# Causal attention of a fused decoder kernel: a step's scores written in one run over whole PSUM banks, both units attended in one run, the output bias added to the residual rows by GpSimd

## Chip, cores and metric

The kernel runs on one core of a Trainium2 chip. The metric is the device time of one execution in microseconds; lower is better. The core has five engines with a queue of instructions each: TensorE (PE in the profile, its weight loads PEld), VectorE (DVE), ScalarE (ACT), GpSimd (POOL) and SyncE (SP), which here only starts transfers.

## The reference, cut to what matters

Two decoder layers over 64 sequences of 64 tokens with 128 features. The change touches one sublayer, the causal self-attention of the second layer (16 heads of 8 features):

```python
def _L1_attn_ref(x, Wq, bq, Wk, bk, Wv, bv, Wo, bo):
    q = split_heads(x @ Wq + bq)
    k = split_heads(x @ Wk + bk)
    v = split_heads(x @ Wv + bv)
    att = jnp.einsum('bhqd,bhkd->bhqk', q, k) * scale
    att = jnp.where(tril, att, -inf)
    att = jax.nn.softmax(att, axis=-1)
    y = jnp.einsum('bhqk,bhkd->bhqd', att, v)
    return y @ Wo + bo
...
x = x + _L1_attn_ref(_layernorm(x, axis=-1), ...)
```

Everything is float32.

## The kernel before, in words

The program is written by hand, engine by engine, one stage after another; engines meet only at semaphores, and each engine works through its own list in order. The stage in question is `causal_attention`. The tokens lie as 32 tiles of 128 rows in the tensor `X`. A step takes two tiles, that is four sequences; there are 16 steps. The four sequences of a step are two units of two sequences.

What a step n does, and on which engine:

- POOL: `combine` adds the routed experts' results of the sublayer before to the two tiles of `X` (three operations, L2197, L2202, L2208); `root` takes the reciprocal root of the norm's variance (L154).
- DVE: `stats` (L141 to L148) and `normed` (L161) are the norm; the normed rows go to `xn`.
- PE: `turn_rows` transposes them (L1945), ACT `rows` copies them to `hT`; PE `project_qk` makes queries and keys (L1953), ACT `copies_q` and `copies_k` spread them over head slots (L2107, L2112), two instructions each; PE `project_v` makes the values (L1961), ACT `spread_v` copies them.
- PE `score`: for one unit, 16 small matmuls of 32 rows by 32 columns write the causal mask's bias over 256 columns of banks 0 to 3 (L1977), and 8 matmuls with 32 rows add the products of queries and keys (L1982). Each float32 matmul appears as two records in the trace. Both units use the same half of the four banks, so a unit's scores can be written only when DVE has read those of the unit before (`less_top`).
- DVE `softmax`: the largest of each row (L2284) and the difference (L2287); ACT `exp` (L2133).
- PE `turn`: four transposes of a quarter of a step's probabilities (L1992), written to the one bank `TURN_BANK`; ACT `copy_turned` copies them out (L2128). A step has four such turns, named by unit and half: 0,0; 0,1; 1,0; 1,1.
- PE `attend`: for one unit, probabilities by values and probabilities by ones (L2009), into `ATTN_BANK`; DVE `normalise` takes the reciprocal (L2292) and multiplies (L2294).
- PE `project`: a matmul of ones by a row that holds the output bias (L2021) starts the sum, two matmuls (L2023) add the output projection; DVE `add` adds the result to `X` (L2299).

`run_steps` writes the order. Its body for step n also works on the norm of later steps and on the end of earlier ones. The order of PE's body before, in a middle step: scores of unit 0; turn 1,0 of step n-1; project n-2; turn 1,1 of n-1; attend unit 0 of n-1; project_qk of n+1; scores of unit 1; project_v of n; turn 0,0 of n; attend unit 1 of n-1; turn 0,1 of n; turn_rows of n+2. Steps 3 to 10 run in a hardware loop with two steps in a turn, the others are written out. The last body and the one before it also make keys, values and queries of the next stage (`next_...`).

## Time and profile before

| | us |
|---|---|
| median of 3 runs | 1831.68 |
| lowest and highest | 1824.25, 1832.2 |
| the profiled execution's own time | 1832.89 |
| its span, from first to last instruction | 1831.1 |
| PE busy in the span | 1726.8 (94%) |
| DVE busy | 1202.5 (66%) |
| ACT busy | 895.7 (49%) |
| POOL busy | 617.2 (34%) |
| mean granted clock of TensorE, share of full speed | 0.982 |

The times in rows of the trace are counted from the start of the span. The stage of the change lies from about 1205 to 1396 us. Busy time leaves out waiting. Matmul records overlap, since one enters the array while the one before drains; the distance from the start of one group to the start of the next says what a group costs on PE, and the record's own length is longer by the drain.

### The profile page before, as it was taken

Reading aid. Unit: us, or ns where it says so; the run is one execution under the profiler, and the core shown is the slowest. Engines: PE = TensorE matmul, PEld = TensorE weight load, DVE = VectorE, ACT = ScalarE, POOL = GpSimd, SP = SyncE. Lnnn points to the kernel's source line nnn. Section 1 sums busy time; section 2 is a strip of 40 time slices with the busy share of each in tenths; the row PEclk is TensorE's granted clock in tenths of the full one; section 3 lists DMA queues with packets and bytes.
Section 4 is the critical chain, followed back from the end, with each engine's and each line's share of the span. In section 5 each row is a group of like instructions: output and inputs, shape, how many; then the busy total and the mean of one; then the engine's idle time right before and its main releaser. Section 6 shows DMA issues by size and latency. Waiting matters only on the chain. (4 is left out here: it accounts for less than half of the span.)

```text
span 1831.1 us, 49181 instructions
## 1 busy us (share of the span) xinstructions
PE 1726.8 (94%) x19304; PEld 1283.1 (70%) x19304; DVE 1202.5 (66%) x2925; ACT 895.7 (49%) x1930; POOL 617.2 (34%) x744
## 2 busy tenths in 40 slices
PE   6999999998999999999799999989998999999778
PEld 5566666666888888888556668857776777777643
DVE  6677777656777778776452223238887777777757
ACT  1444444446666766666332213347774555445324
POOL 2111111112334344343215523343222444444427
PEclk9999999999999999999999999989999999999979
DMA  9300000002444444444410002210010333333301
GB/s 331 92 1 0 0 0 0 1 1 90 142 144 138 143 143 139 148 139 138 132 57 31 32 20 98 99 54 26 29 37 32 97 104 97 97 100 102 103 29 41
DMA packets 176164, 146.81 MB, mean 80 GB/s; under 512 B 12168, under 2 KB 154299, under 8 KB 175506
## 3 DMA queue, kind: packets, MB, share of 16 engines
q1 hardware_dynamic: 172690, 139.12, 23.7%
q0 software_dynamic: 3328, 5.58, 0.9%
q8 instruction: 111, 1.82, 0.4%
q14 instruction: 35, 0.29, 0.1%
HBM read 79.00 MB, written 67.43 MB: 80 GB/s over the span
## 5 line engine op out<-in xcount | busy, mean ns | idle before, releaser
L1061 ACT ACTIVATE xa_probs<-ps,xa_top 128x128 f32<-128x128 f32 x512 | 145.9, 368 | 149.5 <-DVE xa_top L1164 148.5
L154 POOL TENSOR_TENSOR rstd<-var_eps,minus_half 128x2 f32<-128x2 f32 (+1 forms) x116 | 91.9, 792 | 358.0 <-DVE var_eps L148 357.8
L1105 POOL TENSOR_TENSOR xa_probs<-xa_probs,xa_total 128x512 f32<-128x512 f32 x128 | 133.0, 1039 | 200.5 <-DVE xa_total L1159 200.5
L977 PE MATMUL ps<-xa_probsT,xa_kv 128*128 128x512 f32 x256 | 136.7, 616 | 15.7 <-DMA xa_probsT<-turned_blocks 14.5
L1164 DVE TENSOR_REDUCE xa_top<-ps 128x4 f32<-128x512 f32 x128 | 88.3, 690 | 91.3 <-PE ps L968 90.3
L956 PEld LDWEIGHTS ps<-xa_kvT,pack_latent 128*128 128x128 f32 x512 | 97.2, 192 | 65.9 <-issue 56.9
L987 PEld LDWEIGHTS ps<-pack_latent,xa_attnT 128*128 128x128 f32 x1024 | 134.0, 192 | 11.4 <-issue 5.7
L968 PE MATMUL ps<-xa_kvT,xa_qT 128*128 128x128 f32 x1024 | 135.5, 276 | 1.4 <-ACT xa_probs L1061 1.4
L987 PE MATMUL ps<-pack_latent,xa_attnT 128*128 128x128 f32 x1024 | 134.4, 275 | 0.0
L395 PEld LDWEIGHTS ps<-pack_moe,la_hid 128*128 128x128 f32 x1024 | 121.0, 192 | 17.4 <-issue 15.3
L956 PE MATMUL ps<-xa_kvT,pack_latent 128*128 128x256 f32 x512 | 131.5, 382 | 1.4 <-PEq L343 1.4
L382 PE MATMUL ps<-la_h2T,pack_moe 128*128 128x512 f32 x256 | 129.8, 616 | 3.1 <-ACT la_hid L591 3.1
L968 PEld LDWEIGHTS ps<-xa_kvT,xa_qT 128*128 128x128 f32 x1024 | 124.8, 192 | 2.4 <-issue 2.1
L591 ACT ACTIVATE la_hid<-ps,pack_moe 128x512 f32<-128x512 f32 x128 | 86.9, 686 | 80.2 <-PE ps L382 78.4
L395 PE MATMUL ps<-pack_moe,la_hid 128*128 128x128 f32 x1024 | 125.2, 278 | 0.0
L2669 POOL TENSOR_TENSOR ba_probs<-ba_probs,ba_top 128x512 f32<-128x512 f32 x64 | 67.2, 1051 | 142.6 <-DVE ba_top L2736 142.6
L2482 PE MATMUL ps<-ba_inT,pack_latent 128*64 128x128 f32 x1920 | 114.7, 277 | 0.3 <-ACT ba_qT_odd L2595 0.3
L1508 DVE TENSOR_TENSOR rt_mid<-ps,rt_silu 128x512 f32<-128x512 f32 x64 | 44.2, 690 | 106.6 <-ACT rt_silu L1362 106.6
L2482 PEld LDWEIGHTS ps<-ba_inT,pack_latent 128*64 128x64 f32 x1920 | 103.4, 137 | 9.0 <-DVE ba_qT_odd L2746 1.5
L1362 ACT ACTIVATE rt_silu<-ps 128x512 f32<-128x512 f32 x64 | 38.1, 597 | 124.1 <-PE ps L1325 124.1
L1157 DVE TENSOR_REDUCE xa_total<-xa_probs 128x4 f32<-128x512 f32 x128 | 84.1, 657 | 18.3 <-ACT xa_probs L1061 17.3
L1152 DVE STREAM_TRANSPOSE xa_blocks<-xa_probs 128x512 f32<-128x512 f32 x128 | 90.3, 705 | 1.2 <-POOL xa_probs L1105 1.2
(349 smaller groups left out, 3759.7 us busy)
## 6 DMA issues: line engine op xcount, KB each, us to landing
turned_blocks<-xa_blocks SPq DMA_DIRECT2D x128, 256.0 KB, 3.2
xa_probsT<-turned_blocks SPq DMA_DIRECT2D x128, 256.0 KB, 3.0
turned_blocks<-ba_blocks SPq DMA_DIRECT2D x64, 256.0 KB, 2.5
ba_probsT<-turned_blocks SPq DMA_DIRECT2D x128, 128.0 KB, 2.7
expert_weights<-experts_dram SPq DMA_DIRECT2D x8, 768.0 KB, 5.4
result_pairs<-zeros SPq DMA_DIRECT2D x1, 4096.0 KB, 29.4
ca_got<-result_pairs SPq DMA_DIRECT2D x16, 256.0 KB, 2.7
slot_rows<-zeros SPq DMA_DIRECT2D x1, 2880.0 KB, 18.2
```

Source lines behind the costliest of these rows:

```text
L154: pool.tensor_tensor(m.rstd[:, 0:tiles], m.var_eps[:, 0:tiles], m.minus_half[:, 0:tiles], ALU.pow).then_inc(sem.rstd, 1)
L382: pe.matmul(HIDDEN[n % 2], w["w1"][:, n // F0, n % F0, :], h2T[:], start=True, stop=True)\
L395: mm = pe.matmul(out, hid[:, n % 2, f, P * t:P * t + P], w["w2"][:, n, f, :], start=(f == 0), stop=(f == F0 - 1))
L956: mm = pe.matmul(bank(PROJ_BANK + n % 2)[:, NS * a:NS * a + NS], qk_fold[:, 2 * n + a, :], kvT[:, k, :, SEQ:], start=True, stop=True)
L968: mm = pe.matmul(bank(u % 2)[:, KEYS * n:KEYS * n + KEYS], qT[:, k, seq, head:head + 2, :].rearrange("p a q -> p (a q)"), kvT[:, k, seq, : ...
L977: pe.matmul(bank(ATTN_BANK + u % 2), kv[:, k, seq, :], probsT[:, u % SETS].rearrange("p g n q -> p n g q"), start=True, stop=True)\
L987: mm = pe.matmul(bank(OUT_BANK)[:, P * t:P * t + P], attnT[:, t, h, :], vo_fold[:, h, :], start=(h == 0), stop=(h == H - 1))
L1061: exp = act.activation(probs[:, s % 4, n], bank(s % 2)[:, KEYS * n:KEYS * n + KEYS], ACT.Exp, bias=top[:, s % 4, n:n + 1], scale=-1.0)
L1105: pool.tensor_tensor(probs[:, u % 4], probs[:, u % 4], over(total[:, u % 4], 2, KEYS), ALU.mult).then_inc(probs_ready, 1)
L1152: dve.transpose(blocks[:, u % SETS], probs[:, u % 4].rearrange("p n (j k) -> p j n k", k=QUARTER))\
L1164: dve.tensor_reduce(top[:, s % 4], scores, AX.X, ALU.min).then_inc(top_ready, 1)
L2482: mm = pe.matmul(proj_bank(n)[SEQ * seq:SEQ * seq + SEQ, P * h:P * h + P], (w["bq"], w["bk"])[n // 4][:, at:at + DHX], tokens[:, seq], sta ...
```

## The change

- `score(step, k)` handles both units: 16 bias matmuls over all 512 columns of the four banks, then 16 matmuls of queries and keys. `scores_done` rises once a step. The run waits for the subtraction of both units of the step before; that wait stands ahead of the last transpose of `turn 0,0`.
- DVE's `softmax` of unit u reads columns 256u to 256u+255 of the banks.
- PE's order in a body becomes: scores; turn_rows of n+1; turn 0,1 of n-1; project n-2; turn 1,0 of n-1; project_qk of n+1; turn 1,1 of n-1; attend unit 0 and unit 1 of n-1; project_v of n; turn 0,0 of n.
- ACT's order becomes: rows of n+1; copy_turned 0,1 and 1,0 of n-1; exp of unit 0 of n; copy_turned 1,1 of n-1; copies_q and copies_k of n+1; spread_v of n; copy_turned 0,0 of n; exp of unit 1 of n.
- DVE's `stats` is done a step further ahead (step n+3) and at the end of a body, behind `normalise`.
- The bias matmul leaves `project`. Ahead of the steps PE makes the bias as 128 equal rows, ACT copies them to `bias_rows`, and POOL's new `add_bias` adds them to the two tiles of `X` after their norm has read them; DVE's `add` waits for that.

```diff
-                def score(step, k, u):
+                def score(step, k):
...
-                            pe.matmul(bank(g)[QUARTER * c:QUARTER * c + QUARTER, 0:NS], w["ident"][rows, rows],
-                                      over(w["causal_bias"][rows, c % 2, :], 1, 2 * QP), start=True, stop=False)
-                    for b in range(2):
+                            pe.matmul(bank(g)[QUARTER * c:QUARTER * c + QUARTER, :], w["ident"][rows, rows],
+                                      over(w["causal_bias"][rows, c % 2, :], 1, SB * QP), start=True, stop=False)
+                    for b in range(SB):
...
-                def turn(step, u, b):
+                def turn(step, u, b, scored_next=None):
...
+                        if j == J - 1 and scored_next is not None:
+                            score_inputs(scored_next)
...
-                    pe.matmul(bank(ROW_BANK)[:, 0:NS], w["ones"][:], out_bias[:], start=True, stop=False)
                     for t in range(2):
                         mm = pe.matmul(bank(ROW_BANK)[:, P * t:P * t + P], attnT[:, P * t:P * t + P], w["co"][:],
-                                       start=False, stop=(t == 1))
+                                       start=True, stop=True)
...
@@ tensor engine, body(step, k, ahead)
                     if here:
-                        score(step, k, 0)
+                        score(step, k)
...
+                    if ahead >= 1:
+                        turn_rows(later(step, 1), 1 - k)
                     if before:
-                        turn(later(step, -1), 1, 0)
+                        turn(later(step, -1), 0, 1)
                     if has(step, 2):
                         project(later(step, -2), ahead)
                     if before:
+                        turn(later(step, -1), 1, 0)
+                    if ahead >= 1:
+                        project_qk(later(step, 1), 1 - k)
+                    if before:
                         turn(later(step, -1), 1, 1)
...
                     if before:
+                        attend(later(step, -1), 1 - k, 0)
                         attend(later(step, -1), 1 - k, 1)
                     if here:
-                        turn(step, 0, 1)
+                        project_v(step, k)
+                    if here:
+                        turn(step, 0, 0, later(step, 1) if ahead >= 1 else None)
...
@@ scalar engine, body
+                    if ahead >= 1:
+                        rows(later(step, 1), 1 - k)
                     if before:
+                        copy_turned(later(step, -1), 0, 1)
                         copy_turned(later(step, -1), 1, 0)
-                        copy_turned(later(step, -1), 1, 1)
                     if here:
                         exp(step, 0)
+                    if before:
+                        copy_turned(later(step, -1), 1, 1)
...
@@ gpsimd
+                def add_bias(step):
+                    rows = m.X[:, 2 * step:2 * step + 2, :]
+                    pool.wait_ge(ln.normed, 2 * step + 2)
+                    pool.tensor_tensor(rows, rows, over(bias_rows[:], 1, 2), ALU.add).then_inc(bias_added, 1)
...
                 for step in range(4, STEPS):
                     pool.wait_ge(ln.normed, 2 * step)
                     combine(step)
+                    add_bias(step - 2)
                     root(step)
...
@@ vector
                 def add(step):
+                    dve.wait_ge(bias_added, count(step, 1, 1))
                     dve.wait_ge(out_done, count(step, 1, 1))
...
                     if before:
                         normalise(later(step, -1), 1 - k)
+                    if ahead >= 3:
+                        stats(later(step, 3))
```

## Rows read from the trace of the kernel before

**Rows 1.** The page: busy time of each engine over the whole span

```profile
PE 1726.8 (94%) x19304; PEld 1283.1 (70%) x19304; DVE 1202.5 (66%) x2925; ACT 895.7 (49%) x1930; POOL 617.2 (34%) x744
```

**Rows 2.** Windows: length, busy us (and records) of PE, PEld, DVE, ACT, POOL; clock

```profile
1301.01:1310.94 9.93, 9.93 (x272) 7.42 (x268) 8.68 (x16) 7.35 (x16) 3.24 (x5) 1.00 0.08 26
1377.50:1396.30 18.80, 16.41 (x425) 13.04 (x423) 15.37 (x32) 7.70 (x15) 1.01 (x1) 1.00 0.01 3
```

**Rows 3.** Timeline, DVE: the softmax that opens steps 1, 2 and 14, last add

```profile
1234.12 1.23 DVE L2284 TENSOR_REDUCE ca_top<-ps 128x16 f32<-128x1024 f32 x1 [0.32 <-PE ps L1982]
...
1244.97 1.22 DVE L2284 TENSOR_REDUCE ca_top<-ps 128x16 f32<-128x1024 f32 x1
...
1365.16 1.21 DVE L2284 TENSOR_REDUCE ca_top<-ps 128x16 f32<-128x1024 f32 x1
...
1395.89 0.42 DVE L2299 TENSOR_TENSOR X<-ps,X 128x256 f32<-128x256 f32 x1 [0.66 <-PE ps L2023]
```

**Rows 4.** Timeline, PE, one step in the middle: start, length, engine, line

```profile
1303.65 0.71 PE L1977 MATMUL ps<-pack_later_constants,pack_constants 32*32 32x256 f32 x32
1304.30 0.74 PE L1982 MATMUL ps<-ca_kpairs,ca_qpar 32*128 32x128 f32 x16
1304.99 0.65 PE L1992 MATMUL ps<-pack_constants,ca_probs 128*128 128x128 f32 x4
1305.48 0.60 PE L2021 MATMUL ps<-ca_out_bias,pack_constants 128*128 128x256 f32 x2
1305.92 0.61 PE L2023 MATMUL ps<-pack_causal,ca_attnT 128*128 128x128 f32 x4
1306.36 0.63 PE L1992 MATMUL ps<-pack_constants,ca_probs 128*128 128x128 f32 x4
1306.92 0.43 PE L2009 MATMUL ps<-ca_probsT,ca_vheads 128*32 128x64 f32 x16
...
1307.95 1.13 PE L1953 MATMUL ps<-ca_hT,pack_causal 128*128 128x256 f32 x4
1309.01 0.71 PE L1977 MATMUL ps<-pack_later_constants,pack_constants 32*32 32x256 f32 x32
...
1310.33 0.69 PE L1961 MATMUL ps<-pack_causal,ca_hT 128*64 128x64 f32 x16
```

**Rows 5.** Timeline, ACT, the same step

```profile
1307.03 0.60 ACT L2128 ACTIVATE ca_probsT<-ps 128x512 f32<-128x512 f32 x1 [0.75 <-PE ps L1992]
1307.68 1.06 ACT L2133 ACTIVATE ca_probs<-ca_probs 128x1024 f32<-128x1024 f32 x1
1309.12 1.02 ACT L2107 ACTIVATE ca_qpar<-ps,ca_qbias,pack_constants 128x256 f32<-128x256 f32 x2 [0.38 <-PE ps L1953]
1310.03 1.02 ACT L2112 ACTIVATE ca_kpairs<-ps,ca_kbias,pack_constants 128x256 f32<-128x256 f32 x2
```

**Rows 6.** Timeline, DVE, from the last operation before the second softmax on

```profile
1309.36 0.60 DVE L161 TENSOR_SCALAR ca_xn<-X,mean_var,rstd 128x128 f32 x2 [0.44 <-POOL rstd L154]
1310.45 1.22 DVE L2284 TENSOR_REDUCE ca_top<-ps 128x16 f32<-128x1024 f32 x1 [0.49 <-PE ps L1982]
...
1312.92 1.75 DVE L2292 RECIPROCAL ca_rden<-ps 128x256 f32<-128x256 f32 x1
...
1315.30 1.23 DVE L2284 TENSOR_REDUCE ca_top<-ps 128x16 f32<-128x1024 f32 x1 [0.18 <-PE ps L1982]
```

**Rows 7.** Timeline, PE: the first scores of step 0, and what follows

```profile
1220.97 1.17 PE L1977 MATMUL ps<-pack_later_constants,pack_constants 32*32 32x256 f32 x32 [0.60 <-ACT ca_kpairs L2112]
...
1223.24 3.21 PE L1914 MATMUL ps<-pack_latent,ba_inT 128*128 128x512 f32 x4
```

**Rows 8.** All instructions of a line or tile: ns min/median/max, first and last start

```profile
L2208 POOL TENSOR_TENSOR X<-X,ca_got x16: 722/731/741, 1213.6 to 1352.2; 128x256 f32<-128x256 f32 x16
```

**Rows 9.** Timeline of the next stage, DVE, then POOL in the same microseconds

```profile
1410.64 1.32 DVE L2724 TENSOR_SCALAR ba_xn<-X,mean_var,rstd 128x128 f32<-128x128 f32 x2
...
1410.80 1.08 POOL L2669 TENSOR_TENSOR ba_probs<-ba_probs,ba_top 128x512 f32<-128x512 f32 x1 [0.28 <-DVE ba_top L2736]
```

More of the change, by code:

```diff
@@ L1946, in turn_rows, with project_qk @@
                     mm.then_inc(hT_turned, 1)
-                def project_qk(step, k, scored):
+                def project_qk(step, k):
                     pe.wait_ge(hT_ready, count(step, 1, 1))
                     for n in range(2):
-                        if n == 1 and scored is not None:
-                            score_inputs(scored, 1)
                         mm = pe.matmul(bank(QK_BANK)[:, NS * n:NS * n + NS], w["cqk"][:, n, :], hT[:, k, :],
@@ L2028, in body @@
                     here, before = ahead >= 0, has(step, 1)
-                    if not before or ahead == 0:
-                        score_inputs(step, 0)
+                    if not before:
+                        score_inputs(step)
                     if here:
-                        score(step, k, 0)
+                        score(step, k)
                     if not before:
@@ L2035, in body @@
                         next_values(7)
-                        turn_rows(later(step, 1), 1)
+                    if ahead >= 1:
+                        turn_rows(later(step, 1), 1 - k)
                     if before:
-                        turn(later(step, -1), 1, 0)
-                    if before and not has(step, 2):
-                        turn_rows(later(step, 1), 1 - k)
+                        turn(later(step, -1), 0, 1)
                     if not here:
@@ L2045, in body @@
                     if before:
+                        turn(later(step, -1), 1, 0)
+                    if not here:
+                        next_queries(2)
+                    if ahead >= 1:
+                        project_qk(later(step, 1), 1 - k)
+                    if before:
                         turn(later(step, -1), 1, 1)
[L2047 to L2049 removed]
                     if ahead == 0:
                         next_rows()
[L2052 to L2061 removed]
                     if before:
+                        attend(later(step, -1), 1 - k, 0)
                         attend(later(step, -1), 1 - k, 1)
                     if here:
[L2065 removed]
+                        project_v(step, k)
+                    if not before:
+                        pe.wait_ge(kv_copied, 8)
+                    if here:
+                        turn(step, 0, 0, later(step, 1) if ahead >= 1 else None)
                     if ahead == 0:
                         next_queries(0)
[L2068 to L2071 removed]
                     if not here:
@@ L2079, in _ @@
                     .then_inc(offsets_done, 1)
-                pe.matmul(bank(1)[0:1, 0:D], w["c_bias"][:, 2:3], w["co"][:], start=True, stop=False)
-                pe.matmul(bank(1)[0:1, 0:D], w["ones"][0:1, 0:1], w["bo"][0:1, :], start=False, stop=True).then_inc(out_bias_done, 1)
+                pe.matmul(bank(1)[:, 0:D], over(w["c_bias"][:, 2], 1, P), w["co"][:], start=True, stop=False)
+                pe.matmul(bank(1)[:, 0:D], w["ones"][0:1, :], w["bo"][0:1, :], start=False, stop=True).then_inc(out_bias_done, 1)
                 next_context()
@@ L2147, in body @@
                         copy_next_kv(7)
+                    if ahead >= 1:
+                        rows(later(step, 1), 1 - k)
                     if before:
+                        copy_turned(later(step, -1), 0, 1)
                         copy_turned(later(step, -1), 1, 0)
-                        copy_turned(later(step, -1), 1, 1)
-                    if not before:
-                        rows(later(step, 1), 1)
                     if here:
                         exp(step, 0)
+                    if before:
+                        copy_turned(later(step, -1), 1, 1)
                     if ahead >= 1:
                         copies_q(later(step, 1), 1 - k)
-                    if ahead >= 1:
                         copies_k(later(step, 1), 1 - k)
@@ L2172, in body @@
                         act.activation(biased.inT[:].rearrange("p a n -> p (a n)"), next_q_bank(0), ACT.Copy).then_inc(biased.in_ready, 1)
-                    if ahead >= 2:
-                        rows(later(step, 2), k)
                 act.wait_ge(offsets_done, 1)
@@ L2180, in _ @@
                 act.wait_ge(out_bias_done, 1)
-                act.wait_ge(zeroed, 2)
-                act.activation(tiles_of(out_bias[0:1, :]), over(bank(1)[0:1, 0:D], 1, 2), ACT.Copy).then_inc(out_bias_ready, 1)
+                act.activation(bias_rows[:], bank(1)[:, 0:D], ACT.Copy).then_inc(out_bias_ready, 1)
+                act.wait_ge(zeroed, 1)
                 for n in range(4):
@@ L2224, in _ @@
                 root(2)
+                pool.wait_ge(out_bias_ready, 1)
+                add_bias(0)
+                add_bias(1)
                 root(3)
@@ L2228, in _ @@
                     combine(step)
+                    add_bias(step - 2)
                     root(step)
+                add_bias(STEPS - 2)
+                add_bias(STEPS - 1)
                 for first in range(2):
@@ L2307, in body @@
                         softmax(step, 0)
-                    if ahead >= 2 and has(step, 2):
-                        stats(later(step, 2))
                     if not before:
@@ L2321, in body @@
                         normed(later(step, 2))
-                        stats(later(step, 3))
                     if ahead in (0, 1):
```

45 lines of the change are left out of this document (14 added, 31 removed).

## The prediction

> **What bounds the kernel now.** I read the page first: PE is busy 94% of the span, every other engine far less [rows 1]. That is an average over seven stages, so next came the windows of this stage. In a middle step of 9.93 us PE is busy all 9.93 us, DVE 8.68, ACT 7.35, POOL 3.24 [rows 2]. The reader is to see two things: PE sets the pace, and DVE stands only 1.25 us behind it, so no saving on PE above about 1.1 us a step can come through. The timeline of DVE gives the pace over the whole stage: from the first softmax of step 2 at 1244.97 to that of step 14 at 1365.16 are 12 steps in 120.19 us, 10.02 each, 0.09 above the dense step (the hardware loop's turn and small waits); from there to the end of the last `add` at 1396.31 are 31.15 us [rows 3]. The last stretch is looser: PE is busy 16.41 of its last 18.80 us [rows 2]. Then the timeline of PE, for what each piece costs from start to start: scores of a unit 1303.65 to 1304.99, 1.34 us, of which 0.65 the bias matmuls and 0.69 the products, and again 1.32 for the other unit (1309.01 to 1310.33); a turn 0.49; the output bias 0.44; the projection 0.44; a turn that is followed by attention 0.56; attention of a unit 1.03; `project_qk` 1.06; `project_v` to the end of the step 0.61 [rows 2, 4]. Last, ACT and DVE, for who hands over to whom: a copy of turned probabilities starts 0.67 us after its transposes start (1306.36, 1307.03) and takes 0.60 [rows 4, 5]; DVE waited 0.49 and 0.18 us for scores in this step [rows 6].
>
> **The change part by part.** The sum is made against the profiled execution (1832.89, its span 1831.1, 1.8 outside it); that lies 1.2 above the median of 1831.68, and I subtract the gain from the median.
>
> *Scores in one run.* The bias matmuls are 16 in place of twice 16 and twice as wide; the products keep number and width. Per step the columns that stream are the same; what goes is one entry and one exit of the run. The 0.65 us of 256-column bias matmuls hold two rounds of streaming, and a whole-array matmul shows the price of a round: `project_qk` streams two matmuls of 256 columns in 1.06 us [rows 4], at most 0.53 each, of which some 0.10 is again entry and exit, so about 0.43. 256 more columns then cost 0.43 more: 0.65 + 0.43 = 1.08. The products: 0.69 holds two rounds of 128 columns (0.43 by the same price) and 0.25 around them, four rounds give 0.86 + 0.25 = 1.11. Together 2.2 against 2.66, **0.46 less**. Bounds: nothing less (2.66, if no entry is saved), or 2 x 0.43 + 2 x 0.43 = 1.7 with nothing around the streaming.
>
> *Output bias.* PE loses L2021: **0.44 less** [rows 4]. POOL gains one operation of 128x256, the same shape as L2208, 0.73 us [rows 8], on an engine busy 3.24 of 9.93 us [rows 2]: it lies beside everything. It is issued behind `combine`, whose result is wanted by a `stats` that is at least 3 us later in my walk below, and DVE's `add` wants it two steps later. If that cover were gone, the 0.73 would delay `stats` and, behind it in DVE's queue, the next softmax. DVE shares something with POOL: in the next stage two norm applications took 1.32 us while a POOL operation ran over them [rows 9], against 0.60 for the same pair here [rows 6]. In the new order POOL starts its chain when `normed` ends and is done some 4 us later, 5 us before the next `normed`, so I price this at nothing and keep 0.72 per step as a rival. The Trainium skill (GPSIMD Engine Reference, Specifications) says that GpSimd shares its SBUF interfaces with VectorE and contends with its two-port modes and with operations of two SBUF inputs; the traces agree with the 1.32 us, and by this rule any meeting of `add_bias` and `normed` would cost that much. The largest and the difference of a softmax were not touched: 1.22 us with POOL running beside it, as elsewhere [rows 3, 6].
>
> *Both units attended in one run, other order on PE.* One entry into the narrow attention matmuls goes (a turn followed by attention takes 0.56, one that is not 0.49, and leaving costs as much: 0.1 together). One entry into the scores goes, counted above. New PE step by start-to-start prices: scores 2.2, two row transposes 0.25 (half a turn), turn 0.49, project 0.44, turn 0.49, `project_qk` 0.9 (no entry into the scores behind it), turn 0.56, attention 1.93, `project_v` 0.61, turn 0.59: **8.46 us**.
>
> *Waits that the order adds.* There is one transpose bank, and turn 0,1 and turn 1,0 now stand in the same body with only `project` between them. Turn 1,0 can start 0.67 + 0.60 + 0.05 = 1.32 us after turn 0,1 has started; turn and projection fill 0.93. So PE stands **0.4 us** there, and all behind it in its queue. Before, such pairs had the attention or the bias matmul between them. New PE step: 8.46 + 0.4 = 8.86, I take 8.9.
>
> The walk of one step, from the end of the scores (0): DVE's difference of unit 0 is done at 2.6. ACT: copy 0,1 at 0.95 to 1.55, copy 1,0 at 2.25 to 2.85, exp of unit 0 at 2.85, next start 0.95 later (exp takes 1.06, the starts overlap a little [rows 5]), copy 1,1 at 3.8 to 4.4, queries at 4.3, keys at 5.2 to 6.2. PE: turn 1,0 at 1.6, `project_qk` at 2.1, turn 1,1 at 2.95, attention of unit 0 at 3.5, of unit 1 at 4.45 (copy 1,1 is just there), `project_v` at 5.45, turn 0,0 at 6.05, whose last transpose waits for keys until 6.25, scores of n+1 at 6.65 to 8.85. DVE: softmax 0 2.5, `add` 0.35 (0.42 long [rows 3], starts overlap), `normed` 0.5 (0.60 long), softmax 1 2.5 (a softmax is 2.47 from start to start [rows 6]), so both units are read at 5.9; then `normalise` until 8.0 (1312.92 to 1315.30 less the 0.18 wait, 2.2 [rows 6]; its attention is done at 5.6) and `stats` until 8.9. The new scores are ready at 8.9. PE, DVE and the chain over ACT all come out at 8.8 to 8.9. With the 0.09 of before: **9.0 us a step, 1.0 less**. DVE's own work, 8.7 to 8.8, is the floor.
>
> *Head.* Step 0 runs at the low clock: its scores of one unit took 2.27 us [rows 7] against 1.34. The doubled run ends 1.7 later at that clock (0.43 x 2 twice), and what follows it partly at the low clock too; against that unit 1 needs no second run. I put the first softmax of step 1 at 1235.2 instead of 1234.12, that of step 2 at 1244.1 instead of 1244.97. Then 12 steps of 9.0: step 14 at 1352.1 against 1365.16, **13.1 us** earlier. `stats` of step n+3 at a body's end is ready long before its `normed`, so the waits of `normed` for POOL's root (0.44 in a step [rows 6]) vanish; that is inside the DVE walk.
>
> *Tail.* Steps 14, 15 and the last body lose twice 0.9 us of PE work, 1.8 at least. The row for the last 18.80 us has 2.4 us of idle PE, and step 14 has 1 more; at most 5.2 goes. The same walk, with the next stage's pieces at their places, gives 27.1 in place of 31.15: **4.0 us**.
>
> Sum: 13.1 + 4.0 = 17.1, so 1831.7 - 17.1 = 1814.6; I say **1815**. Moving the stage's end moves all later stages, whose work does not change.
>
> **Rivals.**
> - *The scores keep their 2.66 us* (the wider matmuls do not overlap so well, or entries cost nothing). Everything behind the scores is 0.46 later a step: 9.45, gain 0.57 x 12 + 3.5 = 10.3, **1821**. For: the rounds' price is from whole-array matmuls. Against: the same columns stream.
> - *Shared access of DVE and POOL*: `normed` meets `add_bias` or `combine`, 0.72 us more on DVE in each of 13 steps, 9.4 us: **1824**. Against: the 5 us between them.
> - *The keys come too late* (slower). The next scores now wait for keys, which on ACT stand behind exp 0 and copy 1,1, which stand behind DVE's softmax; and as the banks are full, DVE has only `normalise` and `stats` to do meanwhile. In my walk keys are there at 6.2, needed at 6.25. Each 0.1 us later costs 0.1 a step. From 1.0 us later (7.2) the gain per step is gone; at 2.0 later the stage is 12 us longer than now less the tail's 4: **1840**. For it: five hand-overs in a row, none with slack; against it: ACT is busy 7.35 of 8.9 us and the hand-overs' times are read from rows.
> - *The waits dissolve*: a turn's copy comes sooner and the step falls to DVE's floor, 8.8, and the tail gives 5: **1811**.
>
> **How the numbers follow.** Forecast 1812 to 1818: 0.58. Falls to the floor: 0.10. Scores keep their time, or chains a little longer: 0.20, of which a quarter lies within 0.5%. Shared access 0.05, within 0.5%. Late keys 0.07, slower but for 0.01. 0.5% is 9.2 us, about what a measurement of this kernel can tell from no change (its three runs spread over 8 us). Faster than 1822.5: 0.58 + 0.10 + 0.15 = 0.83; same 0.11; slower 0.06. The range reaches from the floor less a part of the runs' spread, 1807, to 1823; outside stand shared access, late keys and some noise. The forecast's own range is 1811 to 1818.
>
> **What would show it.** In the changed profile: first softmaxes 9.0 us apart; L1977 with 512 columns, from its start to that of L1982 1.1 us, and 1.1 to the row transposes; an idle of 0.4 before turn 1,0, released by ACT's L2128; no L2021; POOL with one more 0.73 us operation a step; DVE busy over 95% of a step, its wait for scores under 0.2. Wrong if DVE waits for scores by more than 0.5 each step, if PE's last transpose before the scores waits for L2112, or if L161 grows above 0.35 each.

## The result, and the profile after

The changed kernel takes 1819.3 us (median of 12 runs, 1815.3 to 1825.5) against 1829.7 (12 runs, 1824.3 to 1836.6) before. The ratio is 0.9943 with a 95% interval of 0.9926 to 0.9959, that is 10.4 us less; the forecast was 17.1 less. The interval reaches from 0.41% to 0.74%, on both sides of the 0.5% that the prediction calls faster. The profiled execution took 1815.9 us.

The page of the kernel after, busy time by engine, answers to [rows 1]: PE has 22.9 us less, PEld 15.2 less, POOL 12.2 more; DVE and ACT are as they were.

```profile
PE 1703.9 (94%) x18760; PEld 1267.9 (70%) x18760; DVE 1202.5 (66%) x2924; ACT 894.9 (49%) x1930; POOL 629.4 (35%) x760
```

The windows view of the kernel after, one middle step, with the columns of [rows 2]: the step is 9.05 long, PE again busy nearly all of it, POOL 3.91 where it had 3.24.

```profile
1304.30:1313.35 9.05, 9.01 (x238) 6.75 (x235) 8.55 (x16) 7.36 (x15) 3.91 (x5) 1.00 0.09 29
```

The timeline of PE after, one step, to be held against [rows 4]. L1975 is the bias of the scores, L1980 their products, L1993 a turn, L2023 the projection, L2010 the attention.

```profile
1302.11 1.15 PE L1975 MATMUL ps<-pack_later_constants,pack_constants 32*32 32x512 f32 x32
1303.19 1.17 PE L1980 MATMUL ps<-ca_kpairs,ca_qpar 32*128 32x128 f32 x32
1304.30 0.44 PE L1946 MATMUL ps<-pack_constants,ca_xn 128*128 128x128 f32 x2
1304.57 0.60 PE L1993 MATMUL ps<-pack_constants,ca_probs 128*128 128x128 f32 x4
1305.21 0.71 PE L2023 MATMUL ps<-pack_causal,ca_attnT 128*128 128x128 f32 x4
1305.86 0.66 PE L1993 MATMUL ps<-pack_constants,ca_probs 128*128 128x128 f32 x4
...
1307.79 0.43 PE L2010 MATMUL ps<-ca_probsT,ca_vheads 128*32 128x64 f32 x16
...
1309.93 0.69 PE L1960 MATMUL ps<-pack_causal,ca_hT 128*64 128x64 f32 x16
1310.55 0.68 PE L1993 MATMUL ps<-pack_constants,ca_probs 128*128 128x128 f32 x4
1311.16 1.14 PE L1975 MATMUL ps<-pack_later_constants,pack_constants 32*32 32x512 f32 x32
```

From start to start the scores are 1.08 + 1.11 = 2.19 us. From turn 0,1 (1304.57) to turn 1,0 (1305.86) are 1.29 us; the turn and the projection were priced at 0.93, so 0.36 of it is the stand at the one transpose bank. The rows of PE show no idle time there, since each record's length covers the drain; PEld stands 0.27 us before the projection, for ScalarE's copy of the turned rows (L2095), behind which the copy of turn 0,1 lies in ScalarE's queue.

The timeline of DVE after shows the first softmax of two steps, 8.68 apart here and 9.24 in the step before, and `normed` (L161) at 0.60 for the pair. The timeline of POOL after shows the bias addition (L2209), and that POOL is idle while L161 runs.

```profile
1304.79 1.22 DVE L2287 TENSOR_REDUCE ca_top<-ps 128x16 f32<-128x1024 f32 x1 [0.32 <-PE ps L1980]
...
1307.52 0.60 DVE L161 TENSOR_SCALAR ca_xn<-X,mean_var,rstd 128x128 f32 x2
...
1313.47 1.22 DVE L2287 TENSOR_REDUCE ca_top<-ps 128x16 f32<-128x1024 f32 x1
```

```profile
1308.19 1.05 POOL L2188 TENSOR_TENSOR ca_got<-ca_got,pair_weights 128x512 f32<-128x512 f32 x1 [2.94 <-DVE ca_xn L161]
...
1310.82 0.74 POOL L2209 TENSOR_TENSOR X<-X,ca_bias_rows 128x256 f32<-128x256 f32 x1
```

Up to here everything is as in the walk. The distances between first softmaxes over the whole stage show what is not. From step 2 to step 14, in us: 10.26, 10.55, 10.02, 8.80, 9.24, 8.69, 9.24, 8.68, 8.93, 9.79, 9.49, 8.92; then 13.31 from step 14 to step 15. The hardware loop's steps have a mean of 8.93; around them are steps of 10. PE's timeline says why. Two places, one early and one late:

```profile
1242.85 0.40 PE L2010 MATMUL ps<-ca_probsT,ca_vheads 128*32 128x64 f32 x15
1244.37 0.22 PE L2010 MATMUL ps<-ca_probsT,ca_vheads 128*32 128x64 f32 x1 [1.11 <-issue]
...
1355.23 0.33 PE L2010 MATMUL ps<-ca_probsT,pack_later_constants 128*32 128x64 f32 x9
1358.24 0.32 PE L2010 MATMUL ps<-ca_probsT,pack_later_constants 128*32 128x64 f32 x4 [2.68 <-issue]
```

In the middle of a run of equal matmuls, which wait for nobody, TensorE stands. "issue" is time in which no releaser shows. From matmul start to matmul start the stage has five such places: 1.33 us at 1243.03, 1.73 at 1253.39, 1.12 at 1264.56, 2.90 at 1355.35 and 1.38 at 1369.01, together 8.5. Counted in all the instructions that the trace has of TensorE (matmuls, weight loads, and the waits and register operations between them), the first three lie 513 and 512 apart, the last two 513; in matmuls and weight loads alone it is 500, 500 and 508. I call them stands.

For all comparisons the stage is measured alike: from the first matmul of step 0's scores to the end of the last `add`. It is 175.34 us before (1220.97 to 1396.31) and 166.01 after (1216.93 to 1382.94). That is 9.3 less; the other 7.7 of the difference between the two spans (1831.1, 1814.1) lies outside the stage, in work that the change doesn't touch. The stage began at 1216.2 and 1216.3 in two other kernels that keep the order of before (e2, e7), so the 4.0 us earlier start is no gain of the change. Nor, most likely, are some 2 us of the 9.3: the granted clock of TensorE was 0.50 (1.2 GHz) from 1220 to 1225 us in the profile of before and 1.00 (2.4 GHz) in that of the kernel after, and step 2's softmax came 24.0 us after the stage's start in before, 21.8 in e2 and e7. From step 2's softmax to the stage's end there are 151.3 us before and 145.0 after, 6.4 less; a second profile of the kernel after (e5) has 140.0, 11.3 less. The medians' 10.4 lies between the two. One timed run of a later kernel (e2), 5667 us where its eleven others took 1824 to 1834, is left out of its ratio.

### The profile page after: what moved, and what is told of

The parts are those of the page before. It is cut to its first block and busy times, and to the rows that moved or that the text cites. A ratio compares the mean times of both kernels' runs of the same rounds, so it can differ in the third digit from the quotient of the medians.

```text
span 1814.1 us, 48107 instructions
## 1 busy us (share of the span) xinstructions
PE 1703.9 (94%) x18760; PEld 1267.9 (70%) x18760; DVE 1202.5 (66%) x2924; ACT 894.9 (49%) x1930; POOL 629.4 (35%) x760
## 5 line engine op out<-in xcount | busy, mean ns | idle before, releaser
L987 PEld LDWEIGHTS ps<-pack_latent,xa_attnT 128*128 128x128 f32 x1024 | 133.8, 192 | 12.2 <-issue 6.4
```

Source lines behind the costliest of these rows:

```text
L987: mm = pe.matmul(bank(OUT_BANK)[:, P * t:P * t + P], attnT[:, t, h, :], vo_fold[:, h, :], start=(h == 0), stop=(h == H - 1))
```

## The experiments

"Step" is the mean distance of first softmaxes from step 2 to step 14, "loop" the mean of the six loop steps from step 5 to step 11, "stands" the sum inside the stage of the gaps of over 1.1 us from matmul start to matmul start that are put down to issue. All of these are from one profiled execution; the ratio is from timed runs, against the kernel before timed again on the same chip (its medians were 1828.4 to 1833.7 us), so that the ratios can be compared and the times of different groups not.

| kernel | ratio to before (95%) | step | loop | stage | stands |
|---|---|---|---|---|---|
| before | 1 | 10.02 | 10.03 | 175.3 | 0 |
| after | 0.9943 (0.9926 to 0.9959) | 9.38 | 8.93 | 166.0 | 8.5 |
| after, repeated | 0.9917 (0.9885 to 0.9950) | 9.37 | 8.93 | 162.4 | 4.2 |
| bias on TensorE in the new order | 0.9938 (0.9920 to 0.9955) | 9.90 | 9.12 | 169.4 | 8.7 |
| bias alone changed | 0.9997 (0.9979 to 1.0015) | 10.01 | 10.03 | 172.7 | 0 |
| wide ones | 0.9899 (0.9875 to 0.9922) | 8.97 | 8.93 | 157.3 | 0 |
| wide ones, repeated | 0.9918 (0.9890 to 0.9946) | 8.97 | 8.93 | 157.3 | 0 |

**Bias back on TensorE, in the new order (e1).** The kernel after, but with the output bias as a matmul in `project` again and without `add_bias`.

```diff
@@ project
+                    pe.matmul(bank(ROW_BANK)[:, 0:NS], w["ones"][:], out_bias[:], start=True, stop=False)
                     for t in range(2):
                         mm = pe.matmul(bank(ROW_BANK)[:, P * t:P * t + P], attnT[:, P * t:P * t + P], w["co"][:],
-                                       start=True, stop=True)
+                                       start=False, stop=(t == 1))
```

> The changed kernel with the output bias back in TensorE's project (L2021 of before), the order of the change kept. Two theories on where the gain fell short of the forecast (10.4 us measured, 17.1 worked out). Theory F: TensorE runs out of instructions. In the changed profile it stands still five times in the middle of a run of small matmuls, 1.1 to 2.9 us, at places exactly 512 records apart, and the new order puts all small matmuls of a step behind each other. Theory H: the hand-overs to ScalarE and back take longer than in the walk. For this kernel: the bias matmul (0.44 us) now falls into the stand ahead of turn 1,0, where TensorE waits for ScalarE's copy anyway, so both theories expect little: F expects 0 to 3 us more than the changed kernel (ratio to before 0.994 to 0.997), H, with a longer stand, exactly 0. If the bias matmul were on the path in full, it would be 0.44 x 16 = 7 us more: ratio 0.998.

Its loop steps are 9.12 against 8.93: the bias matmul costs 0.19 of a step there, not the 0.44 of [rows 4]. PE's timeline of this kernel shows where the rest is; it stands between turn 0,1 and turn 1,0, where TensorE has to wait anyway.

```profile
1308.11 0.60 PE L1992 MATMUL ps<-pack_constants,ca_probs 128*128 128x128 f32 x4
1308.75 0.70 PE L2021 MATMUL ps<-ca_out_bias,pack_constants 128*128 128x256 f32 x2
1309.28 0.61 PE L2023 MATMUL ps<-pack_causal,ca_attnT 128*128 128x128 f32 x4
1309.73 0.60 PE L1992 MATMUL ps<-pack_constants,ca_probs 128*128 128x128 f32 x4
```

From turn to turn are 1.62 us, 0.33 more than in the kernel after, though L2021 took 0.53 from its start to that of L2023. The stands came here too, five of them, one of 3.28. The ratio (0.9938) can't be told from that of the change.

**The output bias alone, in the order of before (e2).** `project` loses its L2021, POOL gets `add_bias`, the rest is before.

> The kernel before with nothing changed but the output bias: no L2021 on TensorE, add_bias on GpSimd. TensorE is busy all of a step there, so each step should lose 0.44 us: 16 x 0.44 = 7 us, ratio 0.996. If it takes nothing (ratio 1.000), the step of before is held by something else than TensorE's work. Theory F adds that two instructions fewer a step change nothing about fetching here; theory H has nothing to say.

Ratio 0.9997, and every step from 2 to 14 within 0.03 us of that before. PE's timeline of this kernel, turn 1,0, projection, turn 1,1:

```profile
1297.98 0.65 PE L1993 MATMUL ps<-pack_constants,ca_probs 128*128 128x128 f32 x4
1298.47 0.61 PE L2023 MATMUL ps<-pack_causal,ca_attnT 128*128 128x128 f32 x4
1299.33 0.66 PE L1993 MATMUL ps<-pack_constants,ca_probs 128*128 128x128 f32 x4 [0.24 <-ACT ca_probsT L2128]
```

From turn to turn are 1.35 us; before they were 1.37 (1304.99 to 1306.36 in [rows 4]). The bias matmul is gone and an idle of 0.24 <-ACT stands in its place. Two turns through the one transpose bank can't follow each other faster than the transposes, ScalarE's copy and the hand-over: 0.67 + 0.60 + 0.05. In [rows 4] that wait was covered by overlapping records, and it looked like work.

**The same with that wait filled (e11).** `attend` of unit 0 goes ahead of turn 1,1, so that it lies between the two turns; POOL keeps the bias.

```diff
@@ tensor engine, body
+                        attend(later(step, -1), 1 - k, 0)
                         turn(later(step, -1), 1, 1)
-                        attend(later(step, -1), 1 - k, 0)
```

> e2 (the order of before, output bias on GpSimd) with the attention of unit 0 put ahead of the second turn, so that it lies between the two users of the one transpose bank. If the bias matmul was worth nothing in e2 because TensorE stood there for the copy of the first turn's transposes (1.37 us from turn to turn, filled only by 0.44 of projection): that wait goes, a step of 9.5 to 9.6 instead of 10.01, some 6 us less than e2, a ratio of 0.996 to 0.997. If the steps of before are held by something else (VectorE's norms, or the keys): 10.0 again, and the ratio of e2, 1.000.

1826.24 us (12 runs), ratio 0.9967 (0.9947 to 0.9988), step 9.52, stage 165.1. As expected: 0.49 off each step by exchanging two calls. The intervals of the two ratios (this one, and 0.9979 to 1.0015 of e2) just overlap; it is the steps that tell them apart. PE's timeline of this kernel shows projection and attention between the two turns, 2.06 us apart, and no wait:

```profile
1300.65 0.65 PE L1993 MATMUL ps<-pack_constants,ca_probs 128*128 128x128 f32 x4
1301.13 0.61 PE L2023 MATMUL ps<-pack_causal,ca_attnT 128*128 128x128 f32 x4
1301.67 0.43 PE L2010 MATMUL ps<-ca_probsT,ca_vheads 128*32 128x64 f32 x16
...
1302.71 0.66 PE L1993 MATMUL ps<-pack_constants,ca_probs 128*128 128x128 f32 x4
```

**The ones matmuls over both sequences of a unit (e3, again as e10).** After, with the matmuls of probabilities by ones over 128 columns at a time, half as many. The columns that stream are the same, a step has 412 records of TensorE in place of 476, and the attention of both units 192 in place of 256.

```diff
@@ attend
-                        for part in range(2):
...
+                    at = NS + 2 * SEQ * u
+                    for par in range(2):
+                        for j in range(J):
+                            mm = pe.matmul(bank(ATTN_BANK)[FJ * j:FJ * j + FJ, at:at + 2 * SEQ], w["head_ones"][:, par, :],
+                                           probsT[:, u, :, j, SEQ * par:SEQ * par + SEQ],
+                                           start=(par == 0), stop=(par == 1))
```

> The changed kernel with the attention's matmuls by ones done over both sequences of a unit: 128 columns in place of twice 64, half as many of them, the same columns streamed. TensorE's work in time is the same; its records fall by 64 a step of 476, and the dense run of small matmuls is thinner in instructions. Theory F expects the stands inside the run to shrink or vanish: 4 to 7 us less than the changed kernel, ratio to before 0.990 to 0.992. Theory H expects no difference beyond 1 us: ratio 0.994.

> e3 again, unchanged, beside the other two: a ratio of about 0.990, no stand of over 0.6 us inside the steps of its profile, a mean step of 8.9 to 9.0 and a stage of 157 to 158 us. If e3's one profile was a lucky one and the stands come and go: a mean step of 9.2 or more.

1812.22 us and 1816.62 us (6 runs each). The loop steps are those of after to 0.01 us; outside the loop the steps of 10 are gone, both times. One step there is still long, 9.70 and 9.76 us from step 4 to step 5: a stand of 0.75 and of 0.81 us in the values' projection, above the 0.6 that was expected at most for e10. DVE's timeline of the repeat, first softmax of steps 2 and 14 and the last `add`, to be held against [rows 3]:

```profile
1241.17 1.23 DVE L2290 TENSOR_REDUCE ca_top<-ps 128x16 f32<-128x1024 f32 x1 [0.28 <-PE ps L1980]
...
1348.83 1.22 DVE L2290 TENSOR_REDUCE ca_top<-ps 128x16 f32<-128x1024 f32 x1 [0.93 <-PE ps L1980]
...
1375.71 0.42 DVE L2306 TENSOR_TENSOR X<-ps,X 128x256 f32<-128x256 f32 x1 [0.29 <-PE ps L2026]
```

Twelve steps in 107.66 us, 8.97 each (forecast 9.0), and 27.3 from there to the end (forecast 27.1). The waits of TensorE, of the kernel after (1236 to 1383 us) and then of this one (1230 to 1377), as waiting line, releaser, us in total, times, longest:

```profile
PE ps L2010 <- issue: 6.5, 4, 2.7
PE ps L1993 <- ACT ca_probsT L2121: 1.1, 2, 0.7
PE ps L1960 <- issue: 0.9, 1, 0.9
```

```profile
PE ps L1993 <- ACT ca_probsT L2124: 1.7, 3, 0.8
...
PE ps L2026 <- issue: 0.8, 1, 0.8
PE ps L1960 <- issue: 0.6, 1, 0.6
```

The 7.4 us that L2010 and L1960 waited on "issue" have become 0.6, and the stage is 8.7 shorter. Theory H, by which this edit changes nothing, is out.

**The same edit in the order of before (e7).**

> The kernel before with the same edit of the ones matmuls (128 columns, half as many). Its order never stood still for instructions, so theory F expects 0 (ratio 0.999 to 1.001), although TensorE issues 64 records less a step: it is the run of small matmuls that the edit mends, not their number. If fewer records were worth something by themselves, this kernel would gain the 4 us that the edit brought in the new order (ratio 0.997).

1825.88 us (12 runs), ratio 0.9986 (0.9961 to 1.0011). The steps from 2 to 13 are 9.91 to 10.15, those of before. So the edit by itself is worth nothing that can be measured; what it gave in the new order were the stands. This profile has one of the large kind, 4.99 us, in another place than the attention:

```profile
1355.50 0.66 PE L1992 MATMUL ps<-pack_constants,ca_probs 128*128 128x128 f32 x4
1360.87 0.69 PE L1945 MATMUL ps<-pack_constants,ca_xn 128*128 128x128 f32 x2 [4.71 <-issue]
```

**Ones over all four sequences (e6).**

> As the kernel with the wide ones matmuls, and wider: the matmuls by ones are done once a step over all four sequences, 256 columns, 8 of them in place of the changed kernel's 32. TensorE's records fall by another 32 a step (380 against 412 and 476), the columns stay. Theory F: the stands were gone already with 64 records less; so nothing more, 0 to 1 us, and the steps stay 8.9 to 9.0 us, since DVE is the bound (ratio 0.990). If stands of a kind not seen in the profile remained (the run-to-run spread), up to 3 us more. Theory H: again no difference to the changed kernel (0.994).

1810.32 us (6 runs), ratio 0.9887 (0.9855 to 0.9919). One stand, 2.38 us at 1349.07. Its loop steps are 9.16, 0.2 longer than with the edit of e3; why was not followed up.

**Shifting the records (e4, e12).** After, with tiny matmuls put before step 0: 32 of them, which are 128 records, and 128 of them, 512 records. Their result is overwritten.

```diff
@@ before step 0
+                for _ in range(32):
+                    pe.matmul(bank(0)[0:32, 0:8], w["ident"][0:32, 0:32], w["ident"][0:32, 0:8], start=True, stop=True)
```

> The changed kernel with 32 tiny matmuls (128 records) issued by TensorE ahead of step 0, where it waits for keys anyway. They do no work for the result. Everything that follows in TensorE's instruction stream moves by half a block of 256 records. Theory F expects the stands to leave their places (end of the attention of steps 1, 2, 14, 15) and to appear elsewhere, 128 records earlier in the body, and most likely to become shorter, since the ends of two blocks then do not both fall into the dense run: total 0 to 6 us less than the changed kernel. Theory H expects the same places and the same total within 1 us.

> After's order again with tiny matmuls before step 0, as in e4, but 128 of them (512 records in place of 128), which themselves cost some 6 us before the stage more than e4's 2.1. By F (places in TensorE's stream that lie a whole number of blocks apart, whatever stands there): a shift by 512 puts the places back on the instructions on which they lay in after: stands of 1.1 to 1.7 us in the attention matmuls of steps 2 and 3 and in the value projection of step 4, none at those of e4 in the late written-out steps 12 and 13, mean step 9.35 to 9.4, and the clean steps of the loop at 8.68 to 9.24 as before; a large one late in the stage may come or not, as in after and its repeat. If the shift of e4 did something else (another start of the stage, another clock): the stands of e4 again, or none, and a mean step of 9.9 or of 9.0.

With 128 records (1816.79 us, 6 runs, ratio 0.9933, 0.9906 to 0.9960) nothing stands at 1243 to 1265, where steps of 10.3, 10.6 and 10.0 became 9.7, 8.8 and 9.5. Instead TensorE stands in steps that had run freely, 2.03, 1.55 and 4.77 us. They were expected to be shorter; their sum, 8.4, is that of the kernel after. PE's timeline of two of them:

```profile
1322.86 0.41 PE L2010 MATMUL ps<-ca_probsT,pack_later_constants 128*32 128x64 f32 x16
1325.07 0.43 PE L2010 MATMUL ps<-ca_probsT,ca_vheads 128*32 128x64 f32 x16 [1.81 <-issue]
...
1345.35 0.45 PE L1960 MATMUL ps<-pack_causal,ca_hT 128*64 128x64 f32 x6
1350.35 0.80 PE L1960 MATMUL ps<-pack_causal,ca_hT 128*64 128x64 f32 x10 [4.55 <-issue]
```

With 512 records the stands are back behind the very matmuls of the kernel after: 15 of 16 records into a run of L2010, as at 1242.85, and 9 of 16 into another, as at 1355.23. PE's timeline of this kernel:

```profile
1260.52 0.40 PE L2010 MATMUL ps<-ca_probsT,ca_vheads 128*32 128x64 f32 x15
1262.31 0.22 PE L2010 MATMUL ps<-ca_probsT,ca_vheads 128*32 128x64 f32 x1 [1.39 <-issue]
...
1371.95 0.33 PE L2010 MATMUL ps<-ca_probsT,pack_later_constants 128*32 128x64 f32 x9
1375.78 0.27 PE L2010 MATMUL ps<-ca_probsT,pack_later_constants 128*32 128x64 f32 x4 [3.50 <-issue]
```

Steps 2 to 14 are 10.53, 10.56, 9.74, then 8.80, 9.24, 8.68, 9.23, 8.68, 8.92 in the loop. The padding cost more than expected, 11.9 us where that of e4 took 2.1 and some 6 more were expected; the granted clock was 0.50 from 1222.3 us on, before the padding's end at 1231.1. The whole takes 1833.47 us (10 runs, ratio 1.0010, 0.9988 to 1.0032). Only two of the three early stands pass 1.1 us. The stands are thus set by the place in TensorE's stream, not by what the instructions at that place wait for.

The unit is 256 instructions. The late stands of the kernel after end at TensorE's instruction 23565 and 24078 of the trace, those of e4 at 22285, 22797 and 23309. 23565 less 22285 is 5 times 256, which is no multiple of 512. If the repeated turns of the loop are left out of the count (963 instructions each in these kernels), all 22 stands of over 1.1 us in the seven profiles that have any leave the same remainder by 256, 196 or 197: also those of e1, e6 and e7, whose streams differ, and the large ones.

**Scores in two runs again (e8).** The kernel of e3, with the scores of each unit as a run of its own, one behind the other.

> The kernel with wide ones, and the scores of both units still behind each other, but in two runs of 256 columns, one for each half of the banks, as before the change: 32 bias matmuls in place of 16, two more changes of the array's tiling. In the changed profile the one run takes 1.08 + 1.12 = 2.20 us (forecast 2.2), two runs took 2.66. Walk: the scores are ready 0.46 later, DVE has no more than 0.1 us of slack there, so 0.35 to 0.46 x 14 = 5 to 6.5 us more than the kernel with wide ones (ratio 0.993 to 0.9935), and by theory F perhaps a stand or two more, from 64 records more a step.

1815.45 us (9 runs), ratio 0.9930 (0.9900 to 0.9960). Loop steps 9.27 against 8.93, step 9.39 against 8.97, stage 164.0 against 157.3. PE's timeline of this kernel, both units:

```profile
1313.05 0.71 PE L1976 MATMUL ps<-pack_later_constants,pack_constants 32*32 32x256 f32 x32
1313.69 0.74 PE L1982 MATMUL ps<-ca_kpairs,ca_qpar 32*128 32x128 f32 x16
1314.37 0.71 PE L1976 MATMUL ps<-pack_later_constants,pack_constants 32*32 32x256 f32 x32
1315.01 0.74 PE L1982 MATMUL ps<-ca_kpairs,ca_qpar 32*128 32x128 f32 x16
1315.68 0.44 PE L1946 MATMUL ps<-pack_constants,ca_xn 128*128 128x128 f32 x2
```

2.63 us where one run takes 2.19.

**After repeated (e5), and earlier transfers (e9).** e9 is the kernel of e3 with SP's stores and loads of the next stage's bias tables moved into the loop's time.

> The changed kernel as it is, on the chip of the three kernels below, as their base. Both theories: ratio to before 0.9943 as measured (0.9926 to 0.9959), with stands of TensorE within the runs of small matmuls in its profile, at places 512 records apart.

> The order of e3, with SyncE's stores of the shifted bias tables issued after the gather of step 11 and the loads of the bias values after that of step 14, instead of both behind the last gather; the top weights stay where they were. Estimates from the profiles of the earlier runs. If the large stands of TensorE (2.4 to 5 us, all between about 1338 and 1360 us) come from the instruction transfers lying behind these small packets: none of them here, 0 to 3 us less than e3 again on the same chip and a smaller spread of the times, a ratio of 0.986 to 0.990. If they come from the top weights or from something else: the same as e3, and a profile that may still show one. If the stores, now beside the gathers of the loop, hold up the keys and the values: steps of 9.1 and more in the middle, where e3 has 8.95, and 1 to 3 us more.

The repeat gave 1815.2 us (6 runs), with the three early stands (1.33, 1.46 and 1.39 us, after the same records as before) and without the two late ones. e9 gave 1816.77 us (6 runs), ratio 0.9905 (0.9873 to 0.9937), beside 0.9918 for e10 on the same chip; neither profile has a large stand, and the spread of the times is no smaller (1807.0 to 1820.7 against 1812.9 to 1819.8). It tells nothing about the large stands.

## Why the prediction was right, and where it failed

1819.3 us lies in the range given (1807 to 1823) and above the forecast proper (1812 to 1818). By the number alone the rival of 1821, in which the scores keep their time, is nearer than 1815; its mechanism did not happen. What follows is by mechanism.

**The scores in one run: right in mechanism and size.** 1.08 and 1.11 forecast, 1.08 and 1.11 measured. Splitting them again costs 0.44 on TensorE and 0.42 a step. The rival in which they keep their 2.66 is out.

**The output bias: wrong term.** "PE loses L2021: 0.44 less" is true of TensorE's busy time and false of the step. The step of the reasoning that failed is the first one, "PE is busy all 9.93 us", so PE sets the pace. 0.4 of that time was a round trip through the transpose bank that the bias matmul happened to fill, and e2 shows it: without the matmul no step is shorter, and an idle of 0.24 stands in its place. The same rows could have shown it: two turns of [rows 4] are 1.37 us apart, and the prediction itself works out 1.32 for the shortest distance of two turns, but only for the new order. The sum held all the same, by luck in this term, since for the new order it took off 0.44 and put on a stand of 0.4 at that bank (0.36 measured); keeping the bias on TensorE there costs 0.19. The forecast's sign of that stand, an idle of 0.4 before turn 1,0, doesn't show in the rows of PE.

**The order on PE: right.** Where the 1.1 us of the loop steps came from, by clean loop steps: the bias alone nothing, 10.03 in both; filling the wait at the bank, to 9.52 (e11); the rest of the new order with both attends in one run and `stats` later, to 9.27 (e8, which has the wide ones; in the kernel after these left the loop steps at 8.93); scores in one run, to 8.93. So 0.34 of the 1.1 is the scores' one run, and half a microsecond is the wait that other work between the turns would have filled in the order of before too. How the 0.25 between e11 and e8 divides among its parts was not tried.

**The walk: right.** 9.0 a step forecast, 8.93 in the loop, 8.97 over steps 2 to 14 where nothing stands over 1.1 us; the tail 27.3 for 27.1. From step 2's softmax to the end that is 134.9 us in e3 and 135.0 in e10 for 135.1 forecast. The head was shorter than forecast (step 2's softmax 21.1 us after the scores of step 0 begin in the kernel after, 22.3 to 22.4 in e5, e3 and e10, 23.1 forecast), but this is no saving of the change: the forecast took over the low clock of before's head, and at the full clock the order of before has 21.8 (e2, e7). A stage of 158.2 was forecast; it is 157.3 in e3 and e10.

**The sum: a term was missing.** In the profiled kernel after, steps 2 to 14 take 112.6 us and not 108, the rest 32.3 and not 27.1, less 2.1 of head: 7.8 more than forecast, and 8.5 of stands. The walk had no term for TensorE running out of instructions, because the trace of before has no such stand in these steps. Part of the cause is in the change itself: it put the attention of both units in one run, 256 records in 2.14 us (1307.79 to 1309.93), where before a unit's 128 took 1.03 and other work followed. With 192 records in the same time (e3, e10) the largest stand is 0.8 us.

**That it is the fetching of instructions** the DMA packets show. The DMA view (queue, packets, MB, share) of the kernel after shows for 1235 to 1270 us packets of 16 KB on an instruction queue, and in the loop, 1274 to 1320 us, that queue is not even listed:

```profile
q1 hardware_dynamic: 1088, 1.05, 9.8%
q8 instruction: 5, 0.08, 0.9%
q14 instruction: 2, 0.02, 0.2%
```

```profile
q1 hardware_dynamic: 1360, 1.31, 9.4%
```

The stands too fall only outside the hardware loop. Held against the q8 packets of the same trace, the five of the kernel after are:

| TensorE stands (us) | q8 packet, start to end | TensorE goes on after its end |
|---|---|---|
| 1243.03 to 1244.37 | 1242.06 to 1243.17 | 1.19 |
| 1253.39 to 1255.12 | 1252.82 to 1253.80 | 1.32 |
| 1264.56 to 1265.67 | 1262.98 to 1264.26 | 1.42 |
| 1355.35 to 1358.24 | 1355.76 to 1356.63 | 1.61 |
| 1369.01 to 1370.39 | 1368.05 to 1368.98 | 1.41 |

All 22 stands of over 1.1 us end 1.2 to 1.6 us after such a packet has landed. At none of the 268 block ends (the places of remainder 196 or 197) in the stages of the fourteen profiles, loop left out, does TensorE go on sooner than 1.19 us after one. That TensorE stands for that block is inferred from this and from the places; no record says it.

A stand comes in two ways. In 7 of the 22 TensorE used up a block in 2.0 to 2.5 us: these blocks hold the dense attention, and the fewer records of e3 cure them (outside the loop no block of its stage lasts under 3.1 us; in the order of before none lasts under 3.6). In the other 15 the packet began late, 2.6 to 7.8 us after the last block's end, where the median over all is 0.9; in one of them (e4, 4.77) both came together. Where blocks last longer a late packet costs less: in e3, whose stands of 0.75 and 0.68 us had packets that began 3.1 us late, these blocks took 4.9 and 4.7 us.

The Trainium skill (Runtime: NRT & Kernel Launch, Instruction fetch mechanics) says that an engine's instructions come in blocks of 16 KiB, 256 of them, fetched by its own queue, and that crossing a block is mostly hidden. The packets' size and the 256 agree, and so does "mostly": 246 of the 268 crossings cost less than 1.1 us. The 22 others cost 1.1 to 5.0.

The six stands of 2.4 to 5 us (the kernel after, e1, e4, e6, e7, e12) are at block ends like the rest, with packets that began 4.5 to 7.8 us after the last block's end. All six packets began while SyncE's stores and loads of small packets ran (in the kernel after 1339.9 to 1351.4 and 1353.2 to 1359.1 us), but others that began in such traffic were on time. Why a packet begins late stays open. A large stand can cost more than its length: with five of the six (not e6) the granted clock fell from 1.00 to 0.50 (2.4 to 1.2 GHz), in the stand or within 0.4 us behind it, for 3.4 or 6.8 us.

**The other rivals.** DVE and POOL did not meet: L161 kept its 0.60, POOL being idle then. The keys were not late: the last turn before the scores (L1993 at 1310.55) waits for nobody. The forecast that DVE is busy over 95% and waits less than 0.2 for scores missed: 8.55 of 9.05 is 94%, and every second step waits 0.3 (the 9.24 and 8.68 alternate). POOL has one more operation of 0.73, and L2021 is gone, as said.

**Which version to keep.** The new order with wide ones: 0.9899 and 0.9918, against 0.9943 and 0.9917 for the change as it is. By these ratios alone the difference is not settled. On the chip of e3 (1812.22 us) the two variants of the kernel after, e1 and e4, took 1816.97 and 1816.79; and by the stage (157.3 twice, against 166.0 and 162.4) it is clear.

## What to carry to other kernels

A window in which an engine is busy all the time can hide a wait, since overlapping matmul records and fillers cover it: before pricing the removal of a piece, look whether it lies between two users of one buffer, and compare their distance with the shortest round trip. Exchanging two calls so that real work lies there took 0.49 us off a step, more than the 0.34 of the scores' one run. When many short instructions are gathered into one run, count them: here, outside the loop, TensorE never came from one block of 256 to the next in under 2.87 us, and fewer and wider instructions were worth microseconds where the streamed columns are the same. And before the stages of two profiles are compared, look at the granted clock at their starts: some 2 us went with it here.

## What the runs showed of the hardware

- Outside the loop, TensorE went from one block of 256 instructions to the next no sooner than 1.19 us after a 16 KB packet of queue q8 had landed; such a packet took 0.9 to 1.5 us. The shortest time from one block's end to the next in 14 profiles is 2.87 us (e4). Shifting the stream by 128 records moved the places where it stood, by 512 put them back.
- Two steps of the new order, 952 records of TensorE (963 instructions with the waits), ran in a hardware loop with no instruction packet on that queue for 46 us. The Trainium skill (Runtime: NRT & Kernel Launch, Instruction fetch mechanics) says that a taken branch outside a window of two blocks forces a fetch; the loop was turned here several times without one. In e1, e3 and e9 one packet fell into the loop's time, for four turns.
- In 32-row tiles, 16 bias matmuls of 512 columns take 1.08 us and 16 of 256 columns 0.65: 0.43 for twice the columns. By the same step, an estimate, 0.22 of each run is entry and exit.
- The one transpose bank, with ScalarE's copy of 0.60 us: from the start of a turn to that of the next 1.29 us in the kernel after, 1.35 in e2 and 1.37 in before; between them lay the projection, and in before the output bias too.
